# Two of a chunk's eight quadrant moves issued from ScalarE's queue, in a two-layer graph attention kernel with a final layer norm

## What is computed

```python
def _gat_layer(x, W, adj):
    proj = x @ W
    Wh, Ws = jnp.split(proj, 2, axis=-1)
    scores = Wh @ Ws.T
    a = jax.nn.softmax(scores, axis=-1) * adj
    out = a @ Wh
    out = out + x
    return jax.nn.leaky_relu(out, 0.01)

y = x
for l in range(2):
    y = _gat_layer(y, W_stack[l], adj)
return _layernorm(x + y, axis=-1)
```

## Time and profile before

| | |
|---|---|
| median of 3 runs | 1764.12 us (1759.08 to 1769.03) |
| the profiled execution's own time | 1765.49 us |
| its span, first to last instruction | 1763.6 us |
| TensorE (PE) busy | 1605.7 us, 91% |
| VectorE (DVE) busy | 1291.2 us, 73% |
| GpSimd (POOL) busy | 778.2 us, 44% |
| ScalarE (ACT) busy | 658.7 us, 37% |
| TensorE's granted clock, mean | 0.984 of 2.4 GHz |
| moves: DMAs, data | 2048 of 64 KB |

### The profile page before, as it was taken

The page is one execution under the profiler, slowest core; times in us unless marked ns, Lnnn a source line. Parts: engine busy times, 40 slices in busy tenths (PEclk is TensorE's granted clock), DMA queues, the critical chain, the costliest instruction groups (busy, mean ns, idle before and its releaser), DMA issues.

```text
span 1763.6 us, 23216 instructions
## 1 busy us (share of the span) xinstructions
PE 1605.7 (91%) x8104; PEld 1323.5 (75%) x8104; DVE 1291.2 (73%) x1558; ACT 658.7 (37%) x1175; POOL 778.2 (44%) x679
## 2 busy tenths in 40 slices
PE   7799999999999999998688999999999999999996
PEld 6787787778777787777577777777777777777774
DVE  4668877887768777777447877787787778777774
ACT  4333333343433333443333333333333333333331
POOL 2344444444434344444353444444444444444444
PEclk9999999999999999999899999999999999999998
DMA  5356676666666666677615666666666666666663
GB/s 173 96 155 188 170 192 180 179 180 177 192 173 184 173 187 181 180 202 196 173 35 152 170 170 188 186 175 182 178 175 174 188 191 173 177 183 174 170 193 99
DMA packets 167748, 302.57 MB, mean 172 GB/s; under 512 B 39760, under 2 KB 68432, under 8 KB 167504
## 3 DMA queue, kind: packets, MB, share of 16 engines
q1 hardware_dynamic: 131056, 167.91, 36.1%
q10 hardware_dynamic: 36576, 133.19, 25.4%
HBM read 157.29 MB, written 9.44 MB: 95 GB/s over the span
## 4 chain that ended last, share of the span: by engine, by line
PE 48%; DVE 28%; POOL 9%; SPq 6%; ACT 4%; issue 3%; DMA 2%; ACTq 0%; POOLq 0%
PE banks L392 16%; PE banks L291 8%; PE banks L293 8%; PE banks L292 8%; POOL a_lo L693 8%; PE banks L394 7%; DVE ring L607 7%; DVE neg_max L579 6%; SPq L223 5%; DVE ring L612 4%; DVE weight L598 2%; DMA turned<-ring 1%; DVE rows L620 1%; DVE rows L622 1%; DVE rows L624 1%
## 5 line engine op out<-in xcount | busy, mean ns | idle before, releaser
L693 POOL TENSOR_TENSOR a_lo<-turned,a_hi 128x512 fp32r<-128x512 f32 x512 | 714.8, 1415 | 797.8 <-ACT a_hi L504 795.0
L392 PE MATMUL banks<-wh,a_hi 128*128 128x512 f32 x2048 | 762.8, 410 | 118.5 <-POOL a_lo L693 111.6
L485 ACT ACTIVATE ring<-banks,neg_max 128x1024 f32<-128x1024 f32 x256 | 286.1, 1118 | 911.0 <-DVE neg_max L579 911.0
L392 PEld LDWEIGHTS banks<-wh,a_hi 128*128 128x128 f32 x2048 | 390.8, 191 | 264.0 <-POOL a_lo L693 151.1
L394 PE MATMUL banks<-wh,a_lo 128*128 128x256 f32 x2048 | 580.2, 283 | 0.0
L579 DVE TENSOR_REDUCE neg_max<-banks 128x1 f32<-128x1024 f32 x256 | 309.1, 1207 | 237.3 <-PE banks L293 237.3
L607 DVE SCALAR_TENSOR_TENSOR ring<-ring,weight,load 128x1024 f32<-128x1024 f32 x256 | 405.8, 1585 | 32.3 <-DMA load<-adj 29.8
L291 PE MATMUL banks<-x_t,q_t 128*128 128x512 f32 x1024 | 407.5, 398 | 5.6 <-DVE x_t L543 4.0
L293 PE MATMUL banks<-x_t,q_t 128*128 128x512 f32 x1024 | 403.0, 394 | 0.0
L292 PE MATMUL banks<-x_t,q_t 128*128 128x512 f32 x1024 | 401.4, 392 | 0.0
L394 PEld LDWEIGHTS banks<-wh,a_lo 128*128 128x128 f32 x2048 | 393.2, 192 | 4.9
(11 more groups left out here) (65 smaller groups left out, 723.5 us busy)
## 6 DMA issues: line engine op xcount, KB each, us to landing
turned<-ring SPq DMA_DIRECT2D x2048, 64.0 KB, 2.9
load<-adj ACTq DMA_DIRECT2D x254, 512.0 KB, 4.4
ring<-x SPq DMA_DIRECT2D x8, 512.0 KB, 5.5
rows<-x SPq DMA_DIRECT2D x32, 128.0 KB, 4.6
x_scratch<-rows SPq DMA_DIRECT2D x32, 128.0 KB, 2.4
ring<-x_scratch SPq DMA_DIRECT2D x8, 512.0 KB, 4.9
rows<-x_scratch SPq DMA_DIRECT2D x32, 128.0 KB, 3.3
first_rows<-x SPq DMA_DIRECT2D x32, 128.0 KB, 4.3
```

What stands on the lines that cost most here:

```text
L392: nc.tensor.matmul(psum[:, bank, :], a_hi[:, s, b], wh[:, k].rearrange("p a d -> p (a d)"), start=start, stop=stop, skip_group_check=True)
L485: nc.scalar.activation(ring[:, i % RING, :].rearrange("p (b e) -> p b e", b=2), psum[:, 2 * (i % 2):2 * (i % 2) + 2, :], ACT.Exp, bias=neg ...
L693: nc.gpsimd.tensor_tensor(a_lo[:, j % 2].rearrange("p b (r j) -> p b r j", r=QUADS), as_f32(turned[:, unit % 2, :, b:b + SUB, :]).rearrang ...
```

## The change

Six of a chunk's eight moves stay on SyncE's queue, with their waits. The last two (the last two source quadrants of the second destination quadrant) are issued by ScalarE's queue, at the end of its step: behind the exponential of chunk s and the load of adj, for the same chunk s-4, with the same two waits. The order of the semaphores' counts stays as it is: 64 per quadrant and unit. Steps without an exponential or a load issue them too.

```diff
+        chunk_moves = [(q, r) for q in range(2) for r in range(QUADS)]
+        SP_MOVES, ACT_MOVES = chunk_moves[:6], chunk_moves[6:]
+
+        def move(queue, i, moves):
+            u, c = i // 2 % 2, i % 2
+            for q, r in moves:
+                to = 2 * c + q
+                queue.dma_start(as_f32(turned[QUAD * to:QUAD * (to + 1), u, r]).rearrange("p b j -> p (b j)"),
+                                ring[QUAD * r:QUAD * (r + 1), i % RING, q * BANK:(q + 1) * BANK]
+                                ).then_inc(moved[u][to], 16)
...
             def move_blocks(i):
-                unit, c = i // 2, i % 2
-                u = unit % 2
                 sp.wait_ge(blocks_turned, i + 1)
-                if unit >= 2:
-                    sp.wait_ge(lo_done, SUB * (unit - 1))
-                for q in range(2 * c, 2 * c + 2):
-                    for r in range(QUADS):
-                        sp.dma_start(as_f32(turned[QUAD * q:QUAD * (q + 1), u, r]).rearrange("p b j -> p (b j)"),
-                                     ring[QUAD * r:QUAD * (r + 1), i % RING, (q - 2 * c) * BANK:(q - 2 * c + 1) * BANK]
-                                     ).then_inc(moved[u][q], 16)
+                if i >= 4:
+                    sp.wait_ge(lo_done, SUB * (i // 2 - 1))
+                move(sp, i, SP_MOVES)
...
+            def move_blocks(i):
+                act.wait_ge(blocks_turned, i + 1)
+                if i >= 4:
+                    act.wait_ge(lo_done, SUB * (i // 2 - 1))
+                move(nc.scalar, i, ACT_MOVES)
...
                 m = chunk_at(step - LAG_WEIGH)
-                if m is not None and m + 2 < LAYERS * CHUNKS:
-
-                    act.wait_ge(a_done, m + 1)
-                    load_adj(nc.scalar, m + 2)
+                if m is not None:
+                    if m + 2 < LAYERS * CHUNKS:
+
+                        act.wait_ge(a_done, m + 1)
+                        load_adj(nc.scalar, m + 2)
+                    move_blocks(m)
                 for side in sides_after(step):
                     split_side(side)
```

## The result

The changed kernel takes 1784.62 us (1782.24 to 1787.90, 4 runs) against 1762.93 (1759.08 to 1769.03, 4 runs) of the kernel before: a ratio of 1.0123, interval 1.0095 to 1.0150. The forecast was 1752. It is slower by 1.2%, and the sign was wrong. The profiled execution took 1783.01 us, its span 1781.1, 17.5 over the one before.

What follows compares the result with a forecast made beforehand. TensorE, 91% busy, was taken as the bound, its gaps mostly waits for GpSimd's low halves. Mid-run -3, drain -5, between layers 0, layer 1 +18, layer 0 -22: -12, about 1752 us; 8-in-10 range 1738 to 1786.

Steps and rivals of the forecast that it cites:

- a_hi(1) 0.64 late on a chain with nothing to spare: +0.64 x 28 = +18: Layer 1, a tile's second step: ScalarE's high-half split slips 0.64 us behind the exponential, costing 18 us over 28 tiles.
- product(1) starts at 593.24 instead of 594.03: -0.79 x 28 = -22: Layer 0, a tile's second step: its product starts 0.79 us earlier because VectorE's weighing gets ahead of GpSimd, gaining 22 us.
- the gap before product(0): Layer 0, a tile's first step: TensorE gets a new gap of 0.6 us, waiting for the held-off low half.
- the first few and the last ... left out: Layer 1's +18 us counted 28 tiles, leaving out the first few and the last, where the order is another.
- Between the layers ... 0, bounds -4 and +4: Stretch between the layers: loads freed from SyncE's backlog against later slots and splits, net 0 us, bounds -4 and +4.
- An issue runs on the sequencer while the exponential (1.12) runs, so the first 1.1 us are free: ScalarE, behind the exponential: DMA issues cost nothing for their first 1.1 us, while the exponential runs.
- Mid-run ... I take 3 off: Mid-run splits waiting for late moved blocks: 15 us of waits, mostly covered, so 3 us gained, bounds 0 and 15.
- 8 x 0.63 = 5 off: Drain at the kernel's end: eight of 33 issues leave SyncE's queue at 0.63 us each, gaining 5 us.
- The waits, "nothing": ScalarE's two added waits, for turned blocks and for finished low halves, behind the exponential: no cost.
- c=2 and c=3 covered, "so 0": Layer 1, a tile's third and fourth steps: the late split has 0.5 us to spare, so it costs 0.
- A: Rival in layer 0, a tile's first step: GpSimd keeps its lead over VectorE, 1792 us (smaller form near 1768); chance 0.14.
- B: Rival on both DMA queues: they hold each other up, 0.6 us per step more, 1791 us; chance 0.14.

Runs made afterwards that it cites:

- the q guard: Changed kernel, plus GpSimd waiting in layer 0, at the fourth step of tiles where TensorE also makes the next q, until VectorE has weighed: 1770.11 us.
- the layer-1 order: Kernel before, GpSimd behind the weighing in layer 0, and in layer 1 making first low half before inv_std, second after weighing: 1740.73; with ScalarE's moves in drain 1734.73.

## Why the prediction was wrong

- **"a_hi(1) 0.64 late on a chain with nothing to spare: +0.64 x 28 = +18"**: right in mechanism, too small. The slip was 0.69 per tile (19 us), and long issues, of which SyncE's 1.94 us was a sign, now delay a_hi in four tiles, about 5 us. The layer took 25.1 more.
- **"product(1) starts at 593.24 instead of 594.03: -0.79 x 28 = -22"**: this is the step that failed. It counted every tile of layer 0 alike from one without q. Where there is no q it held (-0.86; the gap before product(0) came larger than forecast, 1.10 for 0.6). At c=3 of tiles with q the same 0.5 us slip, or what follows from it, turned a second race the other way: the earlier trace rows showed the weighing ahead there by 0.04, and the prediction used that row only as the price of a race, not as a place where one is run. The layer gained 9.5; with that race taken out it gains 23.0. This is the largest miss, 13 of 30 us, but not the whole of it: without the race the kernel takes 1770.11, for the 1752 forecast.
- **"the first few and the last ... left out"**: the first tiles were given no cost. The first alone goes from 33.4 to 36.2 us, which makes the +2.9 at the start.
- **"Between the layers ... 0, bounds -4 and +4"**: wrong by 5, of which some 3 can be scatter (the changed kernel with the q guard, the same program there, has 147.6 us). It is a sum of two terms: -5.6 with the moves left out, and some +11 of issues in a chain without cover, a part of either by way of the clock. The sentence "An issue runs on the sequencer while the exponential (1.12) runs, so the first 1.1 us are free" holds only in steps that have an exponential.
- **"Mid-run ... I take 3 off"**: the kernel with the moves left out gained nothing in layer 1 and 1.6 us in layer 0, which is within the scatter. The waits for moved blocks did shrink, as shown above, but those in mid-run were covered. **"8 x 0.63 = 5 off"**, in the drain: 5 to 6 in all kernels that have it, 6.6 with the moves left out.
- **The waits, "nothing"**: right. **c=2 and c=3 covered, "so 0"**: right for the typical tile, whose rise of 0.69 is the gap before product(1) alone.
- **The rivals.** A (GpSimd keeps its lead) didn't occur: the weights take 0.23 in every tile. B's figure (1791) is near the result, but by luck and not by its mechanism: ScalarE's pairs took 1.18 in the median, near the forecast, and the 92 of 254 second moves that took 0.7 us or more left the typical tile's slip at 0.69. The range of 8 in 10 holds the result at its upper edge, in the part that was taken in for A and B, so that is luck too. The Trainium skill (Perfetto Trace Analysis, "DMA Instruction — HWDGE (DVE, Sync)") says that an issuing sequencer locks the descriptor generator for its own use. The 0.87 of a second move that begins together with one of SyncE's agrees with that. But one move per step on ScalarE took 515 ns in the median beside SyncE's, with a minimum of 514, and the loads there still took 335, so the traces show no full exclusion.
- **The chances** don't add up as written: 0.37 and 0.10 make 0.47 for faster, and A and B 0.28 for slower, where 0.48 and 0.27 stand. Nothing else hangs on it.

By the steps: 13 in layer 0, 7 in layer 1, 5 between the layers, 3 of mid-run blocks and 3 at the start, less 1 at the end, make the 30 us from -12 to +17.5. Which part of the c=3 race's turn is ScalarE's slip and which the earlier chain of VectorE was not separated.

## What to carry to other kernels

DMA issues on a compute engine's queue are free up to the length of the instruction that runs meanwhile, and beyond it cost one for one where the chain behind them has no slack (0.69 a tile for 0.69 of slip, in layer 1); ask the question in every stretch, also where that instruction doesn't occur. When a change wins a race between two engines, look for all other places where they start within a few tenths of a microsecond: a shift of 0.5 us turned one race for the kernel and one against it. An explicit wait that orders them is better than a slip that happens to: it gave 1750 us alone, and 1735 with the layer-1 order and the relief where it costs nothing.

## What the runs showed of the hardware

Every 27 us or so TensorE fetches 16 KB of instructions (64 packets for 16208 instructions, 48 for 12112), and at 48 of 61 such fetches in the changed kernel (50 of 61 before) a DMA issue takes 1 to 2 us for 0.59, on whichever queue issues; where both issue, the two end together (22 of 24). On SyncE no harm of it was seen here; on ScalarE it delays the next ACTIVATE: 1.77 us of idle time before a_hi in the row shown, for 0.59 in the typical tile. When a second move on ScalarE's queue begins in the same instant as one of SyncE's, it takes 0.87 us for 0.61 (203 of 204 such in two kernels took 0.7 or more); of the others in the changed kernel a quarter were stretched too, for a reason that stays open.

The moves' median time to landing rose from 2.9 us to 4.0 and 4.2 (SyncE's and ScalarE's) with the change, and no tile is seen to wait for it. It isn't two queues alone: with the moves ahead of the exponential it is 3.4 and 2.6, and with SyncE's six alone 3.3. What sets it was not tested.
